# A graph kernel on one Trainium2 core: the usual path gathered in one block, normalization inside the last hop, results added and stored inside the last step

## The reference

```python
deg_isqrt = deg ** (-0.5)                        # deg: incoming edges, at least 1
h = jnp.maximum(_layernorm(x, axis=-1), 0.0)
x = x + L0(h, deg_isqrt, layer_reg, src, dst)    # 10 hops
h = jnp.maximum(_layernorm(x, axis=-1), 0.0)
x = x + L1(h, ...)                               # 4 steps
...
# L0, one hop                                     # L1, one step
agg = segment_sum(feat[src] * e[:, None], dst)    # m = (emb @ W_msg.T + b_msg).reshape(n, 4, 128)
feat_p = agg * 0.9 + 0.1 * h                      # r = segment_sum(m[src, etype], dst)
feat = feat_p * r_i + (1.0 - r_i) * feat          # emb = gru_cell(r, emb, w_ih, w_hh, b_ih, b_hh)
```

## Time and profile before

| | us |
|---|---|
| median of 3 runs (lowest to highest) | 2458.39 (2457.24 to 2459.94) |
| profiled execution, its own time | 2458.51 |
| its span, first to last instruction | 2456.7 |
| so outside the span | 1.8 |
| TensorE matmuls busy | 2162.5 (88%) |
| VectorE busy | 1385.1 (56%) |
| ScalarE busy | 509.4 (21%) |

### The profile page before, as it was taken

How to read it: one execution, slowest core, us unless ns; L and a number is a source line. 1 busy time by engine, 2 the same in 40 slices (tenths; PEclk the granted TensorE clock), 3 DMA queues, 4 the chain that set the end, 5 groups by cost and what they waited for, 6 DMA issues and landing times.

```text
span 2456.7 us, 40725 instructions
## 1 busy us (share of the span) xinstructions
PE 2162.5 (88%) x14377; PEld 1408.0 (57%) x14888; DVE 1385.1 (56%) x2702; ACT 509.4 (21%) x1123; POOL 235.5 (10%) x517
## 2 busy tenths in 40 slices
PE   4545554599999999999799999999999999999996
PEld 2223222489998989898444565444654446544464
DVE  8878787687777777777722337323363224632243
ACT  4868778300000000000400103100031000210010
POOL 4646555000000000000000000000000000000000
PEclk9656656599999999999899999999999999999998
DMA  2000000100000000005100000000000000000001
GB/s 76 22 33 22 29 26 22 50 2 1 2 1 3 1 2 2 2 2 148 48 1 1 1 1 1 1 1 1 1 1 1 1 1 1 1 1 1 1 1 52
DMA packets 21916, 34.30 MB, mean 14 GB/s; under 512 B 2183, under 2 KB 18174, under 8 KB 21201
## 3 DMA queue, kind: packets, MB, share of 16 engines
q1 hardware_dynamic: 18757, 30.56, 3.6%
q10 hardware_dynamic: 2944, 0.93, 0.2%
HBM read 18.04 MB, written 13.45 MB: 13 GB/s over the span
## 4 chain that ended last, share of the span: by engine, by line
PE 77%; DVE 9%; ACT 6%; issue 3%; ACTq 1%; DVEq 1%; DMA 1%; POOL 0%; POOLq 0%
PE ps L855 43%; PE ps L774 27%; PE ps L807 4%; ACT weighed L517 3%; PE ps L795 2%; ACT packed L510 2%; ACTq L490 1%; DVE marks L1041 1%; ACT words L499 1%; DVE dig L1069 1%; DVE big L1071 1%; PE ps L671 1%; DVEq L1028 1%; PE ps L715 1%; DMA x_after_hops<-x 1%
## 5 line engine op out<-in xcount | busy, mean ns | idle before, releaser
L855 PE MATMUL ps<-slots,m_parts 125*128 125x500 fp8e4 (+1 forms) x5600 | 1084.0, 353 | 1.4 <-DVE slots L1341 1.0
L855 PEld LDWEIGHTS ps<-slots,m_parts 125*128 125x128 f16 x5600 | 546.8, 98 | 487.9 <-issue 0.8
L774 PE MATMUL ps<-parts,big 125*128 125x256 f16 x6125 | 669.5, 273 | 6.1 <-DVEq L1388 3.7
L774 PEld LDWEIGHTS ps<-parts,big 125*128 125x128 fp8e4 x6125 | 591.3, 98 | 63.5
L1341 DVE TENSOR_SCALAR slots<-big 128x3200 int32<-128x3200 int32 (+1 forms) x112 | 244.1, 2183 | 280.5 <-PE ps L855 280.4
L671 PE MATMUL ps<-hot_pair,weighed 125*128 125x228 f16 x1000 | 206.4, 351 | 184.3 <-DVE hot_pair L1043 93.8
L671 PEld LDWEIGHTS ps<-hot_pair,weighed 125*128 125x128 f16 x1000 | 111.5, 118 | 279.2 <-ACT weighed L517 242.6
L517 ACT ACTIVATE weighed<-marks,win_w 125x128 f16<-125x128 f16 x625 | 195.6, 390 | 90.0 <-DVE marks L1041 89.0
L456 ACT ACTIVATE rs<-rs 125x25 f32<-125x25 f32 x3 | 0.7, 225 | 717.7 <-DVE rs L920 717.7
L1443 DVE SCALAR_TENSOR_TENSOR r_parts<-ps,over,r_parts 128x500 f16<-128x500 f32 (+1 forms) x28 | 19.1, 683 | 230.1 <-ACT r_parts L587 230.1
L1450 DVE SCALAR_TENSOR_TENSOR gate_r<-ps,over,gate_r 128x500 f32<-128x500 f32 (+1 forms) x28 | 19.1, 682 | 228.6 <-PE ps L807 228.6
(11 more groups left out here) (204 smaller groups left out, 1337.7 us busy)
## 6 DMA issues: line engine op xcount, KB each, us to landing
packed_counts<-packed SPq DMA_DIRECT2D x16, 625.0 KB, 2.9
big<-packed_counts SPq DMA_DIRECT2D x4, 1600.0 KB, 7.5
...
hd<-in_x SPq DMA_DIRECT2D x1, 1562.5 KB
x_again<-in_x SPq DMA_DIRECT2D x1, 1562.5 KB
x_after_hops<-x SPq DMA_DIRECT2D x1, 1562.5 KB
big<-x_after_hops SPq DMA_DIRECT2D x1, 1562.5 KB
...
```

What stands on the lines that cost most here:

```text
L774: last = pe.matmul(ps[:, n % RING, 0:2 * F], tot_f8[0:Q, c, a, :], both((parts0, parts1)[par], a), start=a == 0, stop=a == TILES - 1)
L855: last = pe.matmul(ps[:, k % 2, 0:SIZES[k] * Q], m_parts[0:Q, a, h, t * F:(t + 1) * F], slots_f8[0:Q, t % 2, 0:SIZES[k], a, 0:Q], start=a ...
```

## The change

The general path and the usual path, which alternated on each engine, become one block each, and on TensorE, VectorE and ScalarE the usual one stands first. Beside that:

- `x2` goes to DRAM in seven blocks, each signalled and stored as soon as its tiles are made, and each with two DMAs: rows 0 to 111 and rows 112 to 124. The load of `x2_back` and the stores of the result are split into these rows too, and `x2_back` is loaded when the first block of the last step has been unpacked.
- `update_scales` moves from the last hop to the one before it, behind tile 3 too. The two `unpack`s move from tile 17 to tiles 9 and 12.
- The roots are taken in three batches (`NORMED`: tiles 0 to 15, 16 to 21, 22 to 24), the first two inside the last hop, and 19 of the 25 `normed` tiles stand there (16 behind tiles 17 to 20, three behind tile 23), three more behind the last tile's statistics, and the last three behind the third batch.
- The `normed` transposes go to banks 5, 6, 7, 0, 1, 2, 3. ScalarE makes the first embedding of three blocks, VectorE that of the other four (`first_low`). TensorE makes the first four messages before these four blocks are out of PSUM.
- The last of the four steps is written out behind a loop of three. TensorE transposes blocks 0 to 2 back behind the second type of the last block, blocks 3 and 4 behind its last type, block 5 behind the gates, and block 6 when its embedding is there. VectorE adds 0 to 2 before `low_sums` of the last block, 3 and 4 behind it, and 5 and 6 at the end.

```diff
+NORMED = [(0, 16), (16, 22), (22, 25)]
+EMB_BANK = [5, 6, 7, 0, 1, 2, 3]
+OUT_BANK = [6, 7, 1, 6, 7, 1, 0]
+ROWS_A = 112
+FIRST_BY_ACT = 3
...
@@ -319,26 +324,43 @@
             sp.wait_ge(s_packed[0], 16 + 8 * NB)
             sp.wait_ge(s_packed[1], 16 + 8 * NB)
             sp.dma_start(x_again[0:Q, :, :].rearrange("p c f -> p (c f)"), x_v).then_inc(s_xa, 16)
+
+            def store_x2(k):
...
+                sp.wait_ge(s_x2, k + 1)
+                for lo, hi in ((0, ROWS_A), (ROWS_A, Q)):
+                    sp.dma_start(x2_dram[lo:hi, a:z], x2[lo:hi, :, :].rearrange("p c f -> p (c f)")[:, a:z]).then_inc(s_x2_out, 16)
+
...
+                sp.wait_ge(s_x2_out, 32 * BLOCKS)
+                for lo, hi in ((0, ROWS_A), (ROWS_A, Q)):
+                    sp.dma_start(x2_back[lo:hi, :, :].rearrange("p c f -> p (c f)"), x2_dram[lo:hi, :]).then_inc(s_x2b, 16)
+
+            def store_results():
+                for k in range(BLOCKS):
+                    a, z = START[k] * F, (START[k] + SIZES[k]) * F
...
-
-            sp.wait_ge(s_x2_out, 16)
-            with sp.If(over_any > 0):
-                sp.wait_ge(s_sacc_m, TILES * STEPS + 1)
...
-            with sp.If(over_any < 1):
-                sp.wait_ge(s_slot, STEPS * BLOCKS * TYPES)
-            sp.dma_start(x2_back[0:Q, :, :].rearrange("p c f -> p (c f)"), x2_dram).then_inc(s_x2b, 16)
-            for k in range(BLOCKS):
-                a, z = START[k] * F, (START[k] + SIZES[k]) * F
-                sp.wait_ge(s_res, k + 1)
-                sp.dma_start(out_v[:, a:z], result[0:Q, :, :].rearrange("p c f -> p (c f)")[:, a:z]).then_inc(s_out, 16)
-            sp.wait_ge(s_out, 16 * BLOCKS)
+                    store_x2(k)
...
+                sp.wait_ge(s_slot, TYPES * (BLOCKS * (STEPS - 1) + 1))
+                load_x2()
+                store_results()
 
...
+                if hops_done:
+                    act.wait_ge(s_ring, hops_done)
+                for k in range(BLOCKS):
+                    act.wait_ge(s_ntr, k + 1)
+                    at = ps[:, EMB_BANK[k], 0:SIZES[k] * Q].rearrange("p (c q) -> p c q", q=Q)
+                    act.activation(emb_parts[:, 0, START[k]:START[k] + SIZES[k], :], at, ACT.Relu, scale=EMB).then_inc(s_eh, 1)
+                    if k < FIRST_BY_ACT:
+                        act.activation(emb[:, START[k]:START[k] + SIZES[k], :], at, ACT.Relu).then_inc(s_emb, 1)
...
                     with act.Fori(0, TILES) as c:
@@ -601,25 +655,6 @@
                         update(TILES * s + c, Q, 0)
                         act.wait_ge(s_epi_m, TILES * s + c + 2)
                         emb_high(c, 1)
-            with act.If(over_any < 1):
-                def next_step():
...
+                pe.wait_ge(s_nrm, START[k] + SIZES[k])
+                for j in range(SIZES[k]):
+                    last = pe.transpose(ps[:, EMB_BANK[k], j * Q:(j + 1) * Q], normed[0:Q, START[k] + j, :], ident[0:Q, 0:Q])
+                last.then_inc(s_ntr, 1)
...
+                        if t == 1 and k == BLOCKS - 1 and not more_steps:
+                            for done in range(3):
+                                pe.wait_ge(s_emb, BLOCKS * STEPS + done + 1)
+                                out_transposes(done)
+
+                if more_steps:
+                    message_when_ready(s + 1, 0)
+                    message_when_ready(s + 1, 1)
+                    block_gates(BLOCKS - 1)
+                    for a in range(2, AHEAD):
+                        message_when_ready(s + 1, a)
+                else:
+                    for done in (3, 4):
+                        pe.wait_ge(s_emb, BLOCKS * STEPS + done + 1)
+                        pe.wait_ge(s_res, done - 2)
+                        out_transposes(done)
+                    block_gates(BLOCKS - 1)
+                    pe.wait_ge(s_emb, BLOCKS * STEPS + 6)
+                    pe.wait_ge(s_res, 3)
+                    out_transposes(5)
+                    pe.wait_ge(s_emb, BLOCKS * (STEPS + 1))
...
+                for k in range(BLOCKS):
+                    if EMB_BANK[k] < RING:
+                        pe.wait_ge(s_ring, HOPS * TILES + EMB_BANK[k] + 1)
+                    normed_transposes(k)
+                pe.wait_ge(s_emb, 3)
+                for a in range(AHEAD):
+                    message_when_ready(0, a)
+                pe.wait_ge(s_emb, BLOCKS)
+                with pe.Fori(0, STEPS - 1) as s:
+                    gnn_step(s, True)
+                gnn_step(STEPS - 1, False)
...
+            def norm_tiles(lo, hi):
+
+                for c in range(lo, hi):
+                    TS(normed[0:Q, c, :], x2[0:Q, c, :], stats[0:Q, c, 0:1], dis[0:Q, c:c + 1],
+                       ALU.subtract, ALU.mult).then_inc(s_nrm, 1)
...
+                def hop(h, par, before, scales_at=None):
 
                     step(TS(coef[0:Q, :], inv_deg[0:Q, :], gain[0:Q, ds(h, 1)], None, ALU.mult))
                     for c in range(TILES):
                         dve.wait_ge(s_acc, before + c + 1)
                         hop_tile(step, ps[0:Q, (par * TILES + c) % RING, :], c, h, (parts1, parts0)[par],
                                  lambda: dve.sem_inc(s_ring, 1)).then_inc(s_parts, 1)
+                        if c == scales_at:
+                            update_scales(step)
...
 
...
+                    if c + 1 == START[BLOCK_OF[c]] + SIZES[BLOCK_OF[c]]:
+                        dve.sem_inc(s_x2, 1)
+                    for n, (lo, hi) in enumerate(NORMED):
+                        if c + 1 == hi:
+                            norm_root(n)
+                        if c == hi:
+                            norm_factor(step, n)
+                    if c in (9, 12):
+                        unpack(0, 0, (9, 12).index(c))
+                    if 17 <= c < 21:
+                        norm_tiles(4 * (c - 17), 4 * (c - 16))
+                    if c >= 23:
+                        norm_tiles(16 + 3 * (c - 23), 19 + 3 * (c - 23))
+                norm_factor(step, 2)
+                norm_tiles(*NORMED[2])
...
-            rsqrt(stats[0:Q, :, 1], EPS, dis[0:Q, :], 3)
-            for c in range(TILES):
-                TS(normed[0:Q, c, :], x2[0:Q, c, :], stats[0:Q, c, 0:1], dis[0:Q, c:c + 1],
-                   ALU.subtract, ALU.mult).then_inc(s_nrm, 1)
-
-            dve.wait_ge(s_x2_out, 16)
...
+            def first_low(k):
+                if k >= FIRST_BY_ACT:
+                    dve.wait_ge(s_eh, k + 1)
+                    dve.wait_ge(s_emb, k)
+                    TS(emb[:, START[k]:START[k] + SIZES[k], :],
+                       ps[:, EMB_BANK[k], 0:SIZES[k] * Q].rearrange("p (c q) -> p c q", q=Q), 0.0, None, ALU.max).then_inc(s_emb, 1)
...
+                    else:
+                        add_results((0, 1, 2))
+                        low_sums(BLOCKS * s + k, SIZES[k] * Q, k % 2)
+                        add_results((3, 4))
+                        meanwhile = None
...
+                else:
+                    add_results((5, 6))
...
+                first_features(step)
+                hops_fast()
+                steps = Chain(dve, s_dve_late)
+                for k in range(2):
+                    first_low(k)
+                messages(0, 0, AHEAD)
+                for k in range(2, BLOCKS):
+                    first_low(k)
+                dve.wait_ge(s_x2_out, 32 * BLOCKS)
+                for k in range(BLOCKS):
```

460 lines of the change are left out of this document (240 added, 220 removed).

## The result

| | before | changed |
|---|---|---|
| median, us (lowest to highest) | 2457.81 (2455.4 to 2459.94) | 2431.39 (2430.09 to 2434.82) |
| ratio of the changed kernel to before, 95% interval | | 0.9895 (0.9878 to 0.9912) |
| profiled execution, its span | 2456.7 | 2428.6 |

The changed kernel is 26.4 us faster. The forecast was 18.0 faster, with a range that ended 3.6 us short of what was measured.

What follows compares the result with a forecast made beforehand. TensorE was taken as the bound, winnable only where it stands still: last hop to first gather, and the store-bound end. Gains of 6.7 and 11.3 us, nothing for the rest, made 18.0: median 2440.4 us, range 2435 to 2446.

Steps and rivals of the forecast that it cites:

- The rest: Skipped general path, `If`s at ends of steps, one step-loop turn less: counted as nothing, bounds 0 and 1 us.
- Rival (d): Written-out fourth step: TensorE stops to get new code, 2.7 us each; kernel slower, 2462 us; chance 0.04.
- `update_scales` a hop earlier: In the hops: VectorE has more per tile one hop earlier, so TensorE's wait grows; 0.4 us lost, 0 to 1.0.
- The first place: Last hop to first gather: 27.6 us becomes 19.2, 8.4 gained; 6.7 after `update_scales` and clock losses, 3.5 to 9.5.
- The clock behind the first gather: Behind the first gather: low clock lasts 4.0 us in place of 1.4, costing 1.3 us, 0 to 2.5.
- The second place: Last gather to span's end: tail behind the embedding 18.6 to 5.3 us, less 2.0; 11.3 gained, 9.5 to 12.5.
- the landing: At the end: the last store of 112 rows takes 2.4 us to land, 2.0 to 2.9.
- The twelve: Twelve transposes ahead of the last gathers, where nothing hides them: cost 2.0 us, 1.3 to 2.5.
- The rule on the rows: Stores: a DMA uses the most engines up to 16 dividing its rows: 5 for 125, 16 for 112, 13 for 13.
- (a): Last hop to first gather: worse order around the messages, so the first place gives nothing; 2447 us; chance 0.08.
- (b): Last hop to first gather: high clock kept and quick copies give 10 us or more; 2436 to 2434; chance 0.10.
- (c): Stores at the end: pieces of 112 and 13 rows aren't faster, gain falls by 2 x 1.6; 2443.6; chance 0.07.

Runs made afterwards that it cites:

- e1: Kernel before, with TensorE's usual path as one block right behind the count and its general code behind that; 2452.54 us against 2457.01, ratio 0.9983.
- e7: Kernel before, with each store of the result split into two DMAs of 112 and 13 rows; 2451.52 us, ratio 0.9973 to before.
- e8: Changed kernel, with two skipped blocks of general code again between TensorE's count and first hop; 2439.24 us, ratio 0.9914 to before.
- e3: Changed kernel, with TensorE's general block in front of its usual one; 2433.13 us, ratio 0.9901 to before.
- e4: Changed kernel, with one more skipped block, of four matmuls, ahead of TensorE's usual block; span 2431.9 us, executed once.
- e6: Changed kernel, with each store of the result one DMA of 125 rows again; 2434.71 us, ratio 0.9905 to before.
- e9: Changed kernel, with TensorE's loop over pairs of hops written out and VectorE's kept; 2424.93 us, ratio 0.9855 to before.
- e10: Changed kernel, with the loops over pairs of hops written out on both TensorE and VectorE; 2426.11 us, ratio 0.9863 to before.
- e12: Changed kernel, with hops and all four steps written out on TensorE alone, and ScalarE copying all seven first embeddings; 2420.45 us, ratio 0.9848 to before.
- e5: Changed kernel, with ScalarE copying all seven blocks of the first embedding out of PSUM in place of three; 2429.64 us, ratio 0.9887 to before.
- e2: Kernel before, with TensorE's two skipped general blocks ahead of the hops made one; span 2448.8 us, executed once.

## Why the prediction was wrong

**The step that failed is "The rest".** It counted the skipped general path as nothing, with 0.5 us for VectorE at the flag and bounds 0 and 1. VectorE's part was right (0.46). TensorE's was not looked at: its two branches of 3.94 and 5.63 us lay one behind the other ahead of the first hop, and only one of them was hidden. That is 5.7 us (e1; 5.1 against e7), or 5.84 (e8). Without it and VectorE's 0.46 the changed kernel's median would be some 2437.6, inside the range. Of the 6.0 us that the profiled execution gained up to T, 5.70 are this, 0.46 are VectorE's, and 0.99 is a flag that happened to be written earlier (in the runs its end lies from 464.65 to 465.97, and once at 467.63, where all work began 2.3 later); against them stand 1.2 us of longer hops, within their scatter of 4 us. The 10.82 us of idle time ahead of line 759 were in the trace of before, put down to VectorE's parts, whose rows show them made 6 us earlier. Rival (d) even priced such stops, from VectorE's 2.7 us, but only for code that the change adds, not for code that it takes out of the way.

**`update_scales` a hop earlier** (-0.4): the hops scatter more than that, so no run here shows it.

**The first place** was right in its mechanism, and its sum came near in part by luck. Forecast and measured behind T: first low part 5.2 and 4.6, first message 6.0 and 5.4, fourth message's low part 13.0 and 11.9, seventh embedding and its low part 17.6 and 16.9, first gather 19.2 and 18.2. The four copies took 2.3 us where 2.4 was forecast. But the sum has four low parts behind the fourth message, where the order that stands ahead of it has five: they took 3.0 us, not 2.2. What was left out there was won ahead of it, since the first message came 0.6 earlier and the four messages took 6.5 us in place of 7.

**The clock behind the first gather** (-1.3, 0 to 2.5): in the profiled execution 0. It was 0.56 in the window from 1180 to 1182 and full behind it, so the low level ended some 1.7 us behind the first gather (a mean of 0.56 between 0.50 and 1.00 is 0.24 us at the high level), and not the 4.0 that I took. The 1.4 that I took for the kernel before were 1.8 by the same reading of its row (0.70 from 1196 to 1198, first gather at 1195.40). In e3, e4 and e8, which do the same work in the same order behind T, it stayed low longer, as here in e4, whose first gather is at 1181.90:

```profile
1182.00:1184.00 2.00, 2.00 (x7) 0.81 (x6) 0.69 (x1) 0.63 (x1) 0.00 (x0) 0.50 0.00 0
1184.00:1186.00 2.00, 2.00 (x7) 0.94 (x7) 0.91 (x2) 0.18 (x1) 0.00 (x0) 0.59 0.00 0
```

By the second row the rise came at 1185.6, 3.7 behind the first gather, about where I had put it. The first step, from the first gather to its last one, takes 301.66 us in the changed kernel and 302.95, 302.67 and 302.96 in e3, e4 and e8. So the term is real, but differs between executions: 0 here, 1.0 to 1.3 there. T to the third step's end is 943.7 to 944.3 in these three and 941.3 in the changed kernel and in e6, with e9 and e10 between (942.4 and 942.9). The rest of the 2.4 to 3.0 lies elsewhere: 0.5 to 0.8 ahead of the first gather, where these three were already at the low level some 6 us behind T and the changed kernel was not, and the remainder mostly at the end of the first step (9.96, 9.32 and 9.90 us to the next step's first gather against 9.11), for which no cause was sought. By those three the first place gains 6.7 to 7.3 us, where I had 7.1.

**The second place**: the tail behind the embedding was forecast at 5.3 and is 5.06, the last embedding comes 8.07 behind the last gather (8.44 before), and the seven transposes cost nothing. Within the tail two errors offset each other: the last transposes and adds end 1.30 behind the embedding (1.85 forecast), and SyncE's last issue ends 1.93 behind them (0.55 forecast), since four issues take 2.49 us; its last wait is then 1.4 us, where 2.4 was forecast for the landing. The twelve cost less than the 2.0 taken: 1.48 us in their row, and the whole last step is 1.4 us longer than the second of e12, which has none (304.02 against 302.64). The lower bound, 1.3, was the better value, since TensorE runs at its high clock there: 0.12 us each, where the row of the low clock has 0.21. The rule on the rows, which the forecast met halfway, holds for the shares in e6 and e7.

**The rivals.** (a) did not occur. (b), 10 or more in the first place, was near in the profiled execution (9.75): its condition came true there, the granted clock being 1.00 in every window from 1160 to 1174, through transposes and messages, but it did not in e3, e4 and e8. It was passed only with ScalarE's copies (13.4 in e5). Its price was added up wrong: 10 us in the first place give 2437, not 2436. (c) is refuted by the shares of 0.68 to 0.89, and by e6's and e7's tails. (d) is refuted: TensorE walked through the written-out step, and in e12 through all hops and steps, without a stop. The Trainium skill (Runtime: NRT & Kernel Launch, "Instruction fetch mechanics") says that a taken branch out of the code that was fetched stalls, and that the fetching of straight code is mostly hidden. The records agree on both: 3.3 to 5.6 us for far branches taken, 0.31 for a near one, and no stop in e12's steps. It was read for the rival, and not for the two taken branches of before.

**What stays open**: why the second of two stops in a row lasts 5.5 to 5.6 us (5.626, 5.506 and 5.632 in before, e7 and e8) and the first or a single one 3.5 to 3.9. The second holds two instruction loads where the first holds one, which goes with the longer time but doesn't say why there are two. The length of the skipped code isn't it, since e2's one jump passes both blocks in 3.68 and e3's passes much more in 3.85. It was not tried apart.
